# Graph attention on one core: the kept block summed by TensorE and copied back by ScalarE, and three small products widened to the whole array

## The reference

```python
q = (x @ Wq + bq).reshape(n, HEADS, DIM_OUT)      # k and v alike
scores = einsum('ehd,ehd->eh', q[src], k[dst]) / sqrt(DIM_OUT)
m = segment_max(scores, dst)
e = exp(scores - m[dst])
z = segment_sum(e, dst)
p = e / maximum(z[dst], 1e-16)
out = segment_sum(v[src] * p[:, :, None], dst)
```

## Time and profile before

| | |
|---|---|
| time, median of 3 runs | 4330.5 us (4315.25 to 4342.56) |
| span of the profiled execution, first to last instruction | 4373.7 us |
| PE / DVE / ACT / POOL busy, whole span | 73% / 78% / 51% / 45% |
| mean granted TensorE clock, whole span | 0.857 |

### The profile page before, as it was taken

One profiled execution on the slowest core, in us unless ns is written; L12 is line 12 of the kernel. 1 busy time (PEld: TensorE's weight loads), 2 busy tenths in 40 slices (PEclk: granted clock), 3 DMA queues, 4 the chain that ended last, 5 costly groups with the idle time before them and its releaser, 6 DMA issues. The chain is left out here.

```text
span 4373.7 us, 55725 instructions
## 1 busy us (share of the span) xinstructions
PE 3187.3 (73%) x12662; PEld 2469.6 (56%) x12662; DVE 3425.8 (78%) x9143; ACT 2219.0 (51%) x5988; POOL 1970.1 (45%) x2404
## 2 busy tenths in 40 slices
PE   4645653666776667677774678898889888988786
PEld 2433332454555545555553567777777777777554
DVE  8999995676777778777786468888888888888766
ACT  3235542443444444344445556656666665666456
POOL 1000003565556556556530166666666666666300
PEclk9767666788888889888887899999999999999988
DMA  2111004566666666666645465565556555665351
GB/s 62 36 52 36 12 24 148 180 195 181 182 189 196 187 186 209 184 193 196 195 123 161 135 174 162 161 167 161 162 165 166 162 162 165 164 163 162 86 120 47
DMA packets 295231, 635.62 MB, mean 145 GB/s; under 512 B 78196, under 2 KB 147122, under 8 KB 294656
## 3 DMA queue, kind: packets, MB, share of 16 engines
q0 software_dynamic: 141312, 463.96, 36.9%
q1 hardware_dynamic: 153602, 168.11, 13.7%
HBM read 587.26 MB, written 44.65 MB: 144 GB/s over the span
## 5 line engine op out<-in xcount | busy, mean ns | idle before, releaser
L2368 POOL DMA_INDIRECT area<-d_xr,col x880 | 894.7, 1017 | 729.2 <-DVE area L2605 285.2
L1931 POOL DMA_INDIRECT low<-d_qv,col x516 | 525.8, 1019 | 395.3 <-DVE at_pv L2101 222.0
L2461 PE MATMUL ms_near_a<-low,ms_hotT 128*128 x1760 | 560.4, 401 | 127.1 <-DVE area L2574 85.6
L1977 PE MATMUL at_out<-at_pv,at_hot 128*128 128x264 f32 x1760 | 576.5, 458 | 44.4 <-DVE area L2143 27.5
L1957 PE MATMUL at_kx<-area,tab_c 128*128 x1760 | 530.5, 432 | 41.1 <-ACT tab_c L2031 34.2
L2462 PE MATMUL ms_near_c<-tab_c,ms_hotT 128*128 x1760 | 549.1, 395 | 0.0
L1931 POOL DMA_INDIRECT tab_c<-d_qv,col x352 | 359.5, 1021 | 252.8 <-DVE at_pv L2101 143.3
L2461 PEld LDWEIGHTS ms_near_a<-low,ms_hotT 128*128 128x128 f32 x1760 | 339.7, 197 | 210.9 <-issue 162.0
L1957 PEld LDWEIGHTS at_kx<-area,tab_c 128*128 128x128 f32 x1760 | 384.7, 221 | 128.0 <-issue 52.2
L1977 PEld LDWEIGHTS at_out<-at_pv,at_hot 128*128 128x128 f32 x1760 | 369.1, 223 | 126.9 <-issue 45.8
L2481 PE MATMUL ms_out<-ms_more,ms_hot 128*128 128x257 f32 x1408 | 374.7, 390 | 76.8 <-DVE ms_hot L2595 73.3
(11 more groups left out here) (358 smaller groups left out, 6659.4 us busy)
## 6 DMA issues: line engine op xcount, KB each, us to landing
tab_c<-by_dst_marks SPq DMA_DIRECT2D x110, 512.0 KB
ms_near_no<-by_src_near SPq DMA_DIRECT2D x110, 224.0 KB
area<-d_xr,col POOLq DMA_INDIRECT x880
d_qv<-low SPq DMA_DIRECT2D x10, 1120.0 KB, 5.0
low<-d_qv,col POOLq DMA_INDIRECT x528
d_xr<-mid_hm SPq DMA_DIRECT2D x5, 1128.8 KB, 5.7
tab_c<-d_qv,col POOLq DMA_INDIRECT x352
first_x<-in_x_dram SPq DMA_DIRECT2D x5, 1120.0 KB
```

Of the source, the lines that this page charges most:

```text
L1931: pool.indirect_dma_start(out=ring[t.slot][:, k, :], out_offset=None, in_=m.d_qv, in_offset=bass.IndirectOffsetOnAxis(ap=col[:, t.h, k, 0: ...
L1977: last = TE.matmul(out[:, p % 2, 0:AW], hot[:, t.h % 2, j, :], pv[:, t.h % 2, j].rearrange("p h d -> p (h d)"), start=(k == 0), stop=(k == ...
L2368: pool.indirect_dma_start(out=far_rows(t, p)[:, k, :], out_offset=None, in_=m.d_xr, in_offset=bass.IndirectOffsetOnAxis(ap=col[:, t.h, SPA ...
L2461: TE.matmul(near_a[:, (SPAN * p + k) % 4, 0:TW], rows, m.tab_a[:, bass.ds(at, TW)], start=True, stop=True)
```

## The change

The sum of the kept block moves from DVE to PE and ACT:

- A register table `base` holds for each step where its kept rows lie: the block's own place when the step before had the same block, else a row block `ZERO` of zeros behind the area (`m.area` grows by 264 columns). `blk` and `keep` shrink from 128 partitions to one.
- PE's `sums` leaves its accumulation group open. A new `total(t, p)`, last in the phase on PE, adds `ident` x (the rows at `base`) into the same bank and closes the group. It waits on `rescaled` in a window's first step and on `summed` for the step before.
- ACT's new `keep_total(t, p)` copies the bank to the block's place and signals `summed`. Its place: steps 0, 1 and 2 lie between the parts of `hot_columns` and `hot_rows`, which are cut in two each; step 3 comes first in the next turn.
- DVE's `add` goes. `rescale` now comes behind `weigh`, and DVE no longer reads `out`. `weigh` and `hot_rows` wait on a new semaphore `spent`, set by `sums`.
- m1 gets 128 columns of weights (120 of them zeros), m2 and m3 get 128 rows (120 of them zeros, or weights of zero).
- Some scratch memory of the sorting and messages stages is moved to make room.

```diff
@@ attention, PE
+                bases = Starts(pe, "at_pe_base", base, ZERO, SG)
                     for k in range(SPAN):
                         j = SPAN * p + k
                         last = TE.matmul(out[:, p % 2, 0:AW], hot[:, t.h % 2, j, :], pv[:, t.h % 2, j].rearrange("p h d -> p (h d)"),
-                                         start=(k == 0), stop=(k == SPAN - 1))
-                    last.then_inc(out_in, 1)
+                                         start=(k == 0), stop=False)
+                    last.then_inc(spent, 1)
+
+                def total(t, p):
+                    if not t.exists():
+                        return
+                    if p == 0:
+                        bases.fetch(t.n * SG, SG)
+                        if t.h % WG == 0:
+                            pe.wait_ge(rescaled, t.window + 1)
+                    if p or t.plus(-1).exists():
+                        pe.wait_ge(summed, t.n * SG + p)
+                    TE.matmul(out[:, p % 2, 0:AW], m.ident[:, :], m.area[:, bass.ds(bases.values(p, 1)[0], AW)], start=False, stop=True).then_inc(out_in, 1)
...
-                        TE.matmul(ps[0:HEADS, 0:2 * WSTEPS], sel[:, :], ends.rearrange("p v k -> p (v k)"), start=True, stop=True).then_inc(m1_in, 1)
+                        TE.matmul(ps[:, 0:2 * WSTEPS], sel[:, :], ends.rearrange("p v k -> p (v k)"), start=True, stop=True).then_inc(m1_in, 1)
...
                         if w:
                             chain(t, w, p)
+                        total(old, p)
@@ attention, ACT
+                def keep_total(t, p, at):
+                    act.wait_ge(out_in, t.n * SG + p + 1)
+                    A.copy(m.acc_l0[:, bass.ds(at[p], AW)], out[:, p % 2, 0:AW]).then_inc(summed, 1)
+
                 def period(t):
+                    old, last = t.plus(-LAG - 1), t.plus(-LAG - 2)
+                    if last.exists():
+                        keep_total(last, SG - 1, [None] * (SG - 1) + starts.values(SG - 1, 1))
+                    at = None
+                    if old.exists():
+                        starts.fetch(old.n * SG, SG)
+                        at = starts.values(0, SG)
                     hot_columns(t.plus(1))
+                    if at:
+                        keep_total(old, 0, at)
+                    hot_columns_end(t.plus(1))
+                    if at:
+                        keep_total(old, 1, at)
                     hot_rows(t.plus(-LAG))
+                    if at:
+                        keep_total(old, 2, at)
+                    hot_rows_end(t.plus(-LAG))
                     weight_sums(t.plus(-LAG))
                     w = window_of(t)
                     if w:
                         weights(w)
@@ attention, DVE
-                def add(t, p, at):
-                    if not t.exists():
-                        return
-                    dve.wait_ge(out_in, t.n * SG + p + 1)
-                    row = m.acc_l0[:, bass.ds(at[p], AW)]
-                    if p or t.plus(-1).exists():
-                        dve.wait_ge(summed, t.n * SG + p)
-                    V.scalar_tensor_tensor(row, row, keep[:, bass.ds(t.n * SG + p, 1)], out[:, p % 2, 0:AW], ALU.mult, ALU.add).then_inc(summed, 1)
...
                     for p in range(SG):
                         mult(t, p)
-                        if p == 0 and old.exists() and old.h % WG == 0:
-                            rescale(old, at[0])
-                        add(old, p, at)
                         if p < 2:
                             weigh(ready, p)
-                        else:
+                        if p == 0 and old.exists() and old.h % WG == 0:
+                            rescale(old, starts.load(old.n * SG, 1)[0])
+                        if p >= 2:
                             score(t, p - 2)
```

More of the change, by code:

```diff
@@ L418, in __init__, with spare @@
         SC = steps_cols(SPAN)
+        def spare(n):
+            m.spare_at[0] += n
+            assert m.spare_at[0] <= m.spare.shape[1]
+            return m.spare[:, m.spare_at[0] - n:m.spare_at[0]]
         if weighed:
@@ L1837, in attention @@
         COLS = BODY
+        ZERO = (NB + 1) * AW
         col = m.at_col
@@ L2038, in hot_rows @@
                     if t.plus(-2).exists():
-                        act.wait_ge(out_in, t.plus(-2).n * SG + SG)
+                        act.wait_ge(spent, t.plus(-2).n * SG + SG)
                     for k in range(G):
@@ L2071, in period @@
                         weights(w)
+                act.wait_ge(c_in, 32)
+                starts = Starts(act, "at_act", off, (NB - 1) * AW, SG)
                 hot_columns(Turn(0, 0))
-                each_turn(act, period, LAG + 1)
+                hot_columns_end(Turn(0, 0))
+                each_turn(act, period, LAG + 2)
             @block.vector
@@ L2080, in _ @@
                 V.tensor_reduce(pick[:, :], halves, axis=AX.X, op=ALU.add).then_inc(made, 1)
-                V.tensor_reduce(sel[:, :], halves.rearrange("p k h -> p h k"), axis=AX.X, op=ALU.add).then_inc(made, 1)
-                V.tensor_copy(selT[:, :, :], m.ident[0:HEADS, 0:HEADS].unsqueeze(1).to_broadcast([HEADS, WSTEPS, HEADS])).then_inc(made, 1)
+                V.tensor_reduce(sel[:, 0:HEADS], halves.rearrange("p k h -> p h k"), axis=AX.X, op=ALU.add).then_inc(made, 1)
+                V.memset(sel[:, HEADS:P], 0.0).then_inc(made, 1)
+                V.tensor_copy(selT[:, :, :], m.ident[:, 0:HEADS].unsqueeze(1).to_broadcast([P, WSTEPS, HEADS])).then_inc(made, 1)
+                V.memset(first[:, :], 0.0).then_inc(made, 1)
+                V.memset(scale[:, :], 0.0).then_inc(made, 1)
                 V.memset(carry[:, :], -BIG).then_inc(made, 1)
@@ L2085, in _ @@
                 V.memset(m.area.rearrange("p (b a) -> p b a", a=AW)[:, :, DIM:AW], 0.0).then_inc(made, 1)
+                V.memset(m.area[:, ZERO:ZERO + DIM], 0.0).then_inc(made, 1)
                 dve.wait_ge(c_in, 32)
                 V.tensor_tensor(keep[:, :], blk[:, 1:1 + SUPER], blk[:, 0:SUPER], ALU.is_equal).then_inc(made, 1)
-                dve.wait_ge(made, 7)
-                starts = Starts(dve, "at_dve", off, (NB - 1) * AW, SG)
+                dve.wait_ge(made, 11)
+                V.tensor_scalar(blk[:, 1:1 + SUPER], blk[:, 1:1 + SUPER], float(AW), -float(ZERO), ALU.mult, ALU.add).then_inc(made, 1)
+                dve.wait_ge(made, 12)
+                V.tensor_tensor(keep[:, :], keep[:, :], blk[:, 1:1 + SUPER], ALU.mult).then_inc(made, 1)
+                dve.wait_ge(made, 13)
+                V.tensor_scalar(base[:, :], keep[:, :], float(ZERO), None, ALU.add).then_inc(made, 1)
+                starts = Starts(dve, "at_dve", off, (NB - 1) * AW, 1)
                 HEAD0, TAIL0 = 0, WSTEPS + 2
@@ L2743, in program @@
             m.first_x = sb_early("first_x", [P, 2, RB, DIM])
+            m.spare, m.spare_at = m.area[:, (NB + 1) * AW:AREA], [0]
             m.late_got, m.late_no = sb_early("late_got", [P, SC * SPAN * 2 * P], I32), sb_early("late_no", [P, SC, SPAN, P], I16)
```

57 lines of the change are left out of this document (29 added, 28 removed).

## The result

The changed kernel takes 4408.1 us (median of 4 runs, 4402.1 to 4417.1), the kernel before took 4322.9 us in 4 runs beside it (4313.3 to 4342.6): a ratio of 1.020, with an interval from 1.017 to 1.024. That is 85 us slower, where 8 us faster (4322) was forecast; 4408 lies inside the range of 8 in 10 (4200 to 4455). The two profiled executions show only part of the 85 us: their spans are 4400.3 and 4373.7 us. The profiled execution of before is a slow one, 51 us above the median of 4322.9 and 31 above the slowest of those 4 runs. So the traces differ by 27 us, and they can show where time goes, but not all 85 us.

The account below looks back on a forecast made before the run. No engine was taken as full: DVE paces quiet turns, DVE and PE await each other in chain turns. 0.25 - 0.40 - 0.40 + 0.40 = -0.15 us a window, -8 us over 55, gives 4322 us; range 4200 to 4455.

Parts of the forecast that it names:

- The quiet turn: Attention window's turn where DVE sets the pace: DVE's 2.13 us a phase gives way to PE's 2.19, +0.25 us.
- phase 0: Chain turn's first phase: DVE is busy throughout, so losing `add` saves 0.40 us a window.
- Phase 1: Chain turn: DVE already waits for m1, so a shorter DVE just waits longer: 0.
- phase 2: Chain turn: DVE waits for m2; `total` ahead of m2 and t2 is covered by PE's waits: 0.
- phase 3: Chain turn's last phase: -0.40 us for `add`, +0.40 taken for `total` at PE's lower clock.
- Nothing in the change touches POOL or the gathers, so I take this lateness as staying: Attention's chain turns: PE's results reach other engines late, 245 us of waits ending at "remote", assumed unchanged.
- The last sentence of the prediction: Would be wrong if late results go away or grow when PE has a third result a phase to signal.
- No relief is lost: Rival: DVE's four `add`s in a chain turn are real time, 88 us saved, 4242 us; chance 0.22.
- The clock stays up: Rival: PE has work where it idled, so its clock stays up, saving 96 us, 4234 us; chance 0.15.
- The copy loop is slower: Rival: `total` waits for ACT's copy, one more late round of 2.3 us a window, 127 us, 4457 us; chance 0.31.
- The widening does nothing by itself: Rival: widening m1, m2 and m3 has no effect alone; no time or chance of its own.
- `rescale`: Placed behind `weigh`, so `total(0)` waits 1.13 us later: hidden by PE's work, or 1.1 us a window if uncovered.

Follow-up runs that it names:

- `before_few_gathers`: The kernel before with the gathers of attention's first 5 turns only, later turns reading stale rows: 3762.2 us (0.988).
- `changed_few_gathers`: The changed kernel with the gathers of attention's first 5 turns only, later turns reading stale rows: 3688.0 us (0.969).
- the model: Both kernels with few gathers, POOL passing on PE's results in order, a 1264 ns memset ahead of each in chain turns: before 4121.2 us, changed 4498.6.
- half the hold: Both kernels with few gathers and PE's chain-turn results held by POOL for 597 ns each: before 3782.6 us (0.994), changed 3846.8 (1.012).
- the mixed kernel: Changed kernel with `add` kept on DVE in chain turns, PE and ACT adding in quiet turns: 1.007; with few gathers and 1264 ns holds 4177.8 us (1.098).
- set 5: Before 4402.5 us; changed with `spent` signalled once a turn 1.017; that with few gathers, results held by POOL and no copy wait 1.028.

## Why the prediction was wrong

**What bounds.** The lengths of the phases were right: DVE's 2.13 us gave way to 1.73, PE's 1.75 to 2.20 (2.19 forecast). The prices held: the copy 387 ns forecast, 376 measured; `total`, two records of a product, 0.45 us of PE's phase. The sum over them was wrong at almost every term. The quiet turn was taken at PE's 2.19, +0.25 us a window; it is -2.1, because PE runs ahead of DVE and can fall behind for a whole turn. PE's arrears are paid in phase 0 of the chain turn, taken at -0.40 because "DVE is busy throughout": it is +2.7. There DVE had finished the `score` that t1 needs 4.27 us before PE started t1, where that was 0.10 us in the kernel before. Phase 1, taken at 0, is -1.1; phase 2, taken at 0 because `total` is "covered", is +1.5; phase 3, taken at -0.40 + 0.40, is -0.5. Together that is +0.5 us a window where -0.15 was forecast.

**The step that failed** is "Nothing in the change touches POOL or the gathers, so I take this lateness as staying", and with it "DVE is busy throughout" for phase 0 and "covered" for phases 1 and 2. The price of late results was not fixed. Set beside `before_few_gathers` and `changed_few_gathers`, where no result is late, a window of before is longer by 28.04 - 20.87 = 7.2 us and one of changed by 28.56 - 19.38 = 9.2 us. So the late results, with all else that differs between the chips, cost 2.0 us a window more than before, and the 1.5 us that the change gains without them are more than eaten. DVE's waits at "remote" before the chain's steps are 362.5 us, where they were 93.7 + 32.8 and 13.6 before the first scans, 140.1 in all; the 118.8 us before `add` went away and were more than paid back. The last sentence of the prediction named this case and gave it no price and no chance.

My theory that PE gives more results and that they come later for it is borne out in the model more than in the result. From m1's start to `carries` it takes 2.93 us in the changed kernel, less than before (4.84), and only from m2 to `maxima` it takes more, 5.00 against 4.11. Held by hand for 1.26 us each, both grow by 1.4 to 1.5 (3.18 to 4.57, 3.80 to 5.32); that is the mark of the count, and the result doesn't bear it at m1. What the runs do show is that a result with the same delay, covered in the kernel before, is bare in the changed one (0 against 2.7 us a window with half the hold), and that PE in arrears costs phase 0 its time (the mixed kernel).

**The rivals.** *No relief is lost* (4242) is near in size where nothing else bounds: 74 us with few gathers, 88 forecast. That is luck, since it put the gain into the chain turn, which stays at 12.3 us; the quiet turn has it, as its own "PE's lead over DVE" allowed. It is void on both kinds of chip, by the gathers (1.002) or by the late results (1.020). *The clock stays up*: the clock did rise, 0.84 to 0.88 here, 0.97 to 1.00 with few gathers, but here the time went up beside it. The Trainium skill's rule (TensorE: Matmul & The Clock Gate, "HAM oscillation"), that work in place of gaps keeps the clock up, agrees with the rows; that time follows doesn't. *The copy loop is slower* (4457) had the direction, and part of the mechanism: PE and DVE wait in one loop, and PE stops before `total` for 69.1 us here, and with results held the wait is worth 56 of 377 us. Its price of 2.3 us a window was too high for that wait and missed the rest. Measured is 0.6 us a window between the two traces. The Trainium skill's advice (Perfetto Trace Analysis, Matmuls) for independent groups in rotating banks bears on this part alone. *The widening does nothing by itself* is right: 0.999.

**The rest.** The window was forecast at 27.6, with 29 for the loop; it is 28.3. PE's wait before m2 fell more than forecast (153.0 to 56.0), that before t2 rose (140.4 to 167.5). `rescale`, taken as hidden or 1.1 us, has 33.9 us of waits before it, 0.65 a window, in phase 0. The register loads, taken at 0, have no run of their own; PE's phase of 2.20 us, 0.01 over the forecast, shows no price.

**Open.** Why results of PE come late in the result and in set 5 and not in the four other sets. What of the loss there is count, bare lateness, copy, PE's arrears or ACT's order: the shares above are of a model with one fixed delay, and the one edit tried where results are late by themselves moved nothing that can be told. Whether the mixed kernel would win there was not tried. And what the identity product costs where the gathers bound (12 us): more PE work in the way of the gathers' release is a guess.

## What to carry to other kernels

Where a profile shows idle time that ends at "remote", don't take it as a constant: look what work each reader has while the result is on its way, and whether the change takes that work away. And don't add up phases by the slower engine of each: an engine that runs ahead can fall behind for a while, and the bill comes at the next place where the other needs it. Moving work off the busiest engine pays only if the hand-overs it adds are cheaper than the work; here 180 us of DVE's work turned into 180 us of DVE's waiting. And time such a change on more than one chip and more than once: the same edit was 1.002 in one set, 1.020 in the result, and 74 us faster once the gathers were out of the way.

## What was not expected of the hardware

- The same kernel takes 3802 to 3805 us on four chips, and 4323 and 4402 us in the result and in set 5. In these two, results of PE reach their readers late, with waits of up to 11.3 us; on the four none does. The chip of the result isn't on record, so chip and time can't be told apart. Not all of it is the attention: behind its last scan the profiled execution of before takes 4373.7 - 2275.0 = 2098.7 us, that of `before_few_gathers`, the same kernel there, 3762.0 - 1889.9 = 1872.1.
- The lateness shows while POOL gathers (1464.01 to 1470.28 above). In the one kernel of set 5 whose stage has hardly a gather it isn't seen, but there POOL also passes on every result. More DMA traffic, 332 GB/s, didn't bring it on a chip without it.
- On the quick chips POOL's issuing of gathers is the bound (1.36 us each, 16 a window), a bound that the first trace hides: there POOL stands for `weigh`.
- A delay of 0.6 us on each result of a chain turn cost the kernel before nothing (20.9 us a window with it, 20.8 without) and the changed one 2.7 us a window.
